# Loads of x with 128 rows per batch instead of 112, the last 16 rows zero

## The chip, the cores and the metric

The kernel runs on one core of a Trainium2 chip. The metric is the device time of one execution in microseconds (us); less is better. Between the two kernels, the median of three runs each is compared.

## What is computed

x has 8 batches of 112 rows of 256 float32 values (896 rows in all). A gated attention over a context and a gated mixture of experts are added to it one after the other. Cut to what matters:

```python
def _layernorm(x): m, v = mean(x), var(x); return (x - m) / sqrt(v + 1e-5)

def xattn(x, ctx):                       # x (8, 112, 256), ctx (8, 375, 256)
    h = einsum('eth,efh->etf', x, ctx)
    return einsum('etf,efh->eth', gelu(h), ctx)

def ffn(x, gate_w, gate_b, w1, b1, w2, b2):
    xf = x.reshape(-1, 256)
    top1 = argmax(xf @ gate_w.T + gate_b, axis=-1)      # one of 8 experts
    for e in range(8):
        y = relu(xf @ w1[e].T + b1[e]) @ w2[e].T + b2[e]
        out = out + where(top1 == e, y, 0)
    return out

x = x + tanh(g_xattn) * xattn(_layernorm(x), ctx_1024)
x = x + tanh(g_ffn)   * ffn(_layernorm(x), ...)
```

## The kernel before, in words

The program has two stages. The first one goes over the 8 batches b; each batch is one tile of 112 rows, a row to a partition. The tile of x lives in `x2[0:112, b, X0:RAW]`; `x2` is 128 partitions by 8 batches by 268 floats (4 floats ahead for mean, variance, 1/std and variance plus eps, 256 of x, 8 for the logits of the gate).

For a batch the work is, in this order: VectorE takes the statistics of x (`stats_x`, L564 and L566); GpSimd makes the inverse deviation (L285, L288); VectorE normalises (`norm_x`, L570); TensorE turns the tile (`turn_xn`, L900) and ScalarE copies it out of PSUM (L449); TensorE makes the scores against the turned context (`scores`, L910, 6 matmuls) and the gate's share from x (`x_logits`, L919, 2 matmuls); ScalarE takes the gelu (L457) and copies shares of the gate (`x_share`, L469; `gate_share`, L463); TensorE multiplies with the context's rows (`attend`, L928, 3 matmuls); VectorE adds the result to x (`add_attention`, L582) and takes the second statistics; GpSimd makes the second inverse deviation; ScalarE's queue stores the 112 rows with their statistics into a table in DRAM (`store_x2`, L474).

TensorE's order is written out by hand (L1005 to L1022): scores(0), turn(1), x_logits(0), and then for each b: scores(b+1), x_logits(b+1), turn(b+2), attend(b). x_logits(b) waits, from b = 2 on, until `add_attention` of batch b-2 is done, since it writes the same PSUM bank (L917). VectorE's order is also by hand (L671 to L711): statistics and normalisation of batches 0 to 2, statistics of batches 3 and 4, normalisation of batch 3, and only then `add_attention(0)`. GpSimd makes 1/std of batches 0 and 1, then a row of constants (L324 to L352), then 1/std of batch 2 and on.

The second stage gathers the rows of each expert from the table by indirect DMA (L381), runs nine blocks of 128 rows through the two matrices of their expert (`up`, L978; `down`, L987), and scatters the result (L386).

All big loads are issued by the SP queue, in the order in which they stand in the code (L243 to L258): x of batch 0, turned context of batch 0 (`load_context_T`, L231), x of 1, turned context of 1, x of 2, context rows of 0 (`load_context_rows`, L234), then **the rest of x, batches 3 to 7, in one load (L249)**, turned context of 2, context rows of 1 and of 2, whole contexts of 3 to 7 (`load_context`, L228), experts 0 and 1. SP issues experts 2 to 7 only after the first gathers have landed (L260 to L267). Each of the loads of x has a semaphore of its own; batches 3 to 7 share `x_in[3]`.

The loads of x move 112 rows: 3 loads of 112 rows of 1,024 bytes, and one load of 112 rows of 5 x 268 x 4 = 5,360 bytes (batches 3 to 7 laid out as `x2` has them, with the pads). All other loads of SP have 128 rows: 3,000 bytes a row for a turned context, 3,168 for context rows, 6,168 for a whole context, 8,192 for an expert's matrix.

Of the kernel before, what the change touches and what calls it, by code (L numbers as in the profile page):

```python
# [19 lines left out]
P = 128  # L20
# [10 lines left out]
B, S, D = 8, 112, 256  # L31
CTX = 375
E, H = 8, 1024
# [6 lines left out]
MEAN, VAR, RSTD, VEPS, X0 = 0, 1, 2, 3, 4  # L40
RAW = X0 + D
# [5 lines left out]
HEAD = 3  # L47
# [9 lines left out]
def gated_cross_attention_moe(nc, x, x_rest, ctx, small, w1t, w2t, b2, out):  # L57
    x2_dram = nc.dram_tensor("x2_rows", (TOKENS, ROW), F32, kind="Internal").ap()
    with ExitStack() as stack:
        def sb(name, shape, dt=F32):  # L60
            return stack.enter_context(nc.sbuf_tensor(name, shape, dt))
# [4 lines left out]
        def sem(name):  # L66
            return stack.enter_context(nc.semaphore(name))
# [27 lines left out]
        x2 = sb("x2", [P, B, ROW + E])  # L95
# [81 lines left out]
        x_in = [sem("x_in0"), sem("x_in1"), sem("x_in2"), sem("x_in3")]  # L177
# [47 lines left out]
        @block.sync  # L225
        def _(sp):
            def load_context(b):
                sp.dma_start(cxs[:, b, :], ctx[b]).then_inc(cx_in[b], 16)  # L228

            def load_context_T(b):  # L230
                sp.dma_start(cxT[:, b, :], ctx[b, :, 0:KD * CTX]).then_inc(cxT_in[b], 16)  # L231

            def load_context_rows(b):
                sp.dma_start(cx[:, b, :], ctx[b, :, KD * CTX:CW]).then_inc(cx_in[b], 16)  # L234

            def load_expert(e):
                sp.dma_start(w1[:, e, :], w1t[e]).then_inc(w1_in[e], 16)
                sp.dma_start(w2[:, e, :], w2t[e]).then_inc(w2_in[e], 16)

            def load_x(b):  # L240
                return sp.dma_start(x2[0:S, b, X0:RAW], x[b * S:(b + 1) * S])  # L241

            load_x(0).then_inc(x_in[0], 16)  # L243
            load_context_T(0)
            load_x(1).then_inc(x_in[1], 16)
            load_context_T(1)
            load_x(2).then_inc(x_in[2], 16)
            load_context_rows(0)
            sp.dma_start(x2[0:S, HEAD:B, :], x_rest).then_inc(x_in[3], 16)  # L249
            load_context_T(2)  # L250
            load_context_rows(1)
            load_context_rows(2)
            for b in range(3, B):
                load_context(b)

            load_expert(0)
            sp.dma_start(b2b[:, 0:D], b2[0:D].partition_broadcast(P)).then_inc(b2_in[0], 16)
            load_expert(1)  # L258

            sp.wait_ge(xnT_done, B)  # L260
            sp.wait_ge(xgT_done, 1)
            sp.wait_ge(first_in[1], 16)
            sp.wait_ge(xg_in[0], 16)
            load_expert(2)
            sp.dma_start(b2b[:, D:E * D], b2[D:E * D].partition_broadcast(P)).then_inc(b2_in[1], 16)
            for e in range(3, E):
                load_expert(e)  # L267
# [905 lines left out]
```

## Time and profile before

| what | us |
|---|---|
| median of 3 runs (lowest to highest) | 112.1 (110.88 to 112.54) |
| the profiled execution's own time | 111.79 |
| its span in the trace | 110.0 |
| outside the span | 1.79 |
| TensorE matmul busy | 100.7 (92% of the span) |
| VectorE busy | 53.5 (49%) |
| GpSimd busy | 39.9 (36%) |
| ScalarE busy | 28.6 (26%) |

The span is the stretch from the first to the last recorded instruction; all times in rows count from its start. "PE" is TensorE's matmul side, "PEld" its weight load, DVE is VectorE, ACT ScalarE, POOL GpSimd, SP the sync engine that issues the big loads; a q behind a name is the queue of that engine. L910 is line 910 of the kernel. The names in the rows are those of memory tensors: `x` is the tile `x2`, `region` the tile that holds the contexts, `w` the experts' matrices (in whose last parts the normalised x and the gelu lie for a time), `bank` is PSUM.

### The profile page before, as it was taken

The page shows a single profiled execution, that of the slowest core. Times are in us where ns is not written, and L with a number is a line of the kernel's source. Part 1 is how long each engine was busy: PE and PEld are TensorE (multiplying, and loading weights), DVE is VectorE, ACT ScalarE, POOL GpSimd, SP SyncE. Part 2 cuts the span into 40 slices and gives each one's busy share as a digit, 9 for nine tenths or more (in the row PEclk, how much of TensorE's full clock was granted, in tenths as well). Part 3 has the DMA queues.
Part 4 walks back from the last instruction along what each step waited for, and adds up shares of the span by engine and source line. Part 5 has one row for each costly group of instructions (what it writes and reads, how often), then busy time and mean ns, then how long its engine had stood idle before and what let it go on. Part 6 is the DMA issues. An engine that isn't in the chain of part 4 may idle for free.

```text
span 110.0 us, 2150 instructions
## 1 busy us (share of the span) xinstructions
PE 100.7 (92%) x704; PEld 92.7 (84%) x705; DVE 53.5 (49%) x204; ACT 28.6 (26%) x91; POOL 39.9 (36%) x97
## 2 busy tenths in 40 slices
PE   5999899999999997799999999999999999999900
PEld 5998669999988895799989999899999998998600
DVE  0461578669689884796555332344133241333010
ACT  5616143212351440152302303223032140220000
POOL 3276386353664937700330557030030030300330
PEclk9999999999999999999999999999999999999996
DMA  3999999999995202599999999999992010010101
GB/s 80 316 331 246 404 419 422 404 427 426 413 414 202 86 0 65 128 352 359 368 416 402 419 420 365 415 426 426 432 419 114 7 44 0 0 40 6 46 19 35
DMA packets 6734, 28.36 MB, mean 258 GB/s; under 512 B 1149, under 2 KB 2511, under 8 KB 4672
## 3 DMA queue, kind: packets, MB, share of 16 engines
q1 hardware_dynamic: 4688, 25.09, 58.2%
q0 software_dynamic: 864, 2.12, 6.3%
q10 hardware_dynamic: 1168, 0.98, 2.8%
q8 instruction: 7, 0.11, 0.4%
q14 instruction: 7, 0.06, 0.1%
HBM read 26.33 MB, written 2.11 MB: 259 GB/s over the span
## 4 chain that ended last, share of the span: by engine, by line
PE 71%; DMA 11%; DVE 6%; issue 3%; POOL 2%; SPq 2%; ACTq 0%; ACT 0%; POOLq 0%; DVEq 0%
PE bank L978 29%; PE bank L987 26%; DMA x<-in_x_rest 8%; PE bank L928 6%; PE bank L910 5%; DMA region<-x_rows,from_row 3%; PE bank L960 2%; PE bank L919 2%; DVE x L582 1%; SPq L241 1%; PE bank L900 1%; POOL out_rows L386 1%; DVE stats L589 1%; SPq L231 1%; DVE region L791 1%
## 5 line engine op out<-in xcount | busy, mean ns | idle before, releaser
L978 PE MATMUL bank<-region,w 128*128 128x128 f32 x288 | 34.7, 277 | 0.3 <-ACT region L485 0.3
L978 PEld LDWEIGHTS bank<-region,w 128*128 128x128 f32 x288 | 33.8, 192 | 0.8 <-ACT region L485 0.4
L987 PE MATMUL bank<-w,region 128*128 128x256 f32 x144 | 32.6, 379 | 0.0
L987 PEld LDWEIGHTS bank<-w,region 128*128 128x128 f32 x144 | 26.7, 190 | 3.2
L520 ACT ACTIVATE region<-bank,smalls 128x128 f32<-128x128 f32 x40 | 12.5, 363 | 39.9 <-PE bank L978 38.5
L386 POOL DMA_INDIRECT out_rows<-region,to_row x9 | 8.9, 989 | 33.9 <-DVE region L813 32.4
L797 DVE TENSOR_SCALAR region<-bank,smalls 128x128 f32<-128x128 f32 x32 | 9.7, 346 | 13.8 <-PE bank L978 13.4
L381 POOL DMA_INDIRECT region<-x_rows,from_row x9 | 9.3, 1032 | 15.7 <-DMA region<-x_rows,from_row 12.2
L813 DVE SCALAR_TENSOR_TENSOR region<-bank,tg,region 128x256 f32<-128x256 f32 (+1 forms) x9 | 4.4, 484 | 19.0 <-PE bank L987 19.0
L910 PEld LDWEIGHTS bank<-xnT,region 128*125 128x125 f32 x96 | 11.4, 188 | 2.2 <-issue 1.6
L910 PE MATMUL bank<-xnT,region 128*125 128x120 f32 x96 | 12.0, 275 | 0.8 <-issue 0.7
L928 PE MATMUL bank<-region,w 125*112 125x264 f32 x48 | 12.1, 388 | 0.0
L928 PEld LDWEIGHTS bank<-region,w 125*112 125x112 f32 x48 | 7.8, 177 | 1.5
L457 ACT ACTIVATE w<-bank 125x336 f32<-125x336 f32 x8 | 3.6, 450 | 12.0 <-PE bank L910 12.0
L994 PE MATMUL bank<-still 128*128 128x128 f32 x22 | 5.1, 419 | 1.1 <-DVE still L671 1.1
L582 DVE SCALAR_TENSOR_TENSOR x<-bank,tg,x 112x264 f32<-112x264 f32 x8 | 3.9, 488 | 3.5 <-PE bank L928 3.5
L791 DVE TENSOR_SCALAR region<-region 128x256 f32<-128x256 f32 (+1 forms) x8 | 3.6, 452 | 3.6 <-DMA region<-x_rows,from_row 3.6
L994 PEld LDWEIGHTS bank<-still 128*128 128x128 f32 x22 | 4.6, 318 | 0.8 <-DVE still L671 0.8
L564 DVE BATCH_NORM_STATS2 stats<-x 112x6 f32<-112x256 f32 x8 | 3.4, 422 | 3.7 <-DMA x<-in_x 2.1
L570 DVE TENSOR_SCALAR w<-x,mv 112x256 f32<-112x256 f32 x8 | 3.3, 418 | 3.7 <-POOL mv L288 3.7
L288 POOL TENSOR_TENSOR x<-x,power 112x1 f32<-112x1 f32 x8 | 4.5, 561 | 0.6
L288 POOL TENSOR_TENSOR mv<-mv,power 112x1 f32<-112x1 f32 x8 | 4.4, 553 | 0.6
(118 smaller groups left out, 85.7 us busy)
## 6 DMA issues: line engine op xcount, KB each, us to landing
w<-in_w1t SPq DMA_DIRECT2D x8, 1024.0 KB, 23.3
w<-in_w2t SPq DMA_DIRECT2D x8, 1024.0 KB, 26.5
region<-in_ctx SPq DMA_DIRECT2D x5, 771.0 KB, 13.2
region<-in_ctx SPq DMA_DIRECT2D x3, 396.0 KB, 9.1
region<-in_ctx SPq DMA_DIRECT2D x3, 375.0 KB, 4.2
x_rows<-x ACTq DMA_DIRECT2D x8, 113.8 KB, 6.4
b2b<-in_b SPq DMA_DIRECT2D x1, 896.0 KB
x<-in_x_rest SPq DMA_DIRECT2D x1, 586.2 KB, 8.3
```

The source lines that it names most:

```text
L288: return pool.tensor_tensor(v[:, 2:3], v[:, 3:4], power[0:S, :], ALU.pow)
L381: return pool.indirect_dma_start(out=to, out_offset=None, in_=x2_dram, in_offset=bass.IndirectOffsetOnAxis(ap=idx, axis=0), bounds_check=T ...
L386: return pool.indirect_dma_start(out=out, out_offset=bass.IndirectOffsetOnAxis(ap=idx, axis=0), in_=rows, in_offset=None, bounds_check=TOK ...
L520: act.activation(hidT[:, q, 2 * k + r, :], hT_ps[k][:, r * P:(r + 1) * P], ACT.Relu, bias=b1[:, bass.ds(e * KH + 2 * k + r, 1)]).then_inc( ...
L582: dve.scalar_tensor_tensor(out=x2[0:S, b, X0:ROW + E], in0=at_ps[b % 2][0:S, 0:DL], scalar=tg[0:S, 0:1], in1=x2[0:S, b, X0:ROW + E], op0=A ...
L791: dve.tensor_scalar(xgn[:, q, :], rows[:, X0:ROW], rows[:, MEAN:MEAN + 1], rows[:, RSTD:RSTD + 1], ALU.subtract, ALU.mult).then_inc(xgn_ok, 1)
L797: dve.tensor_scalar(hidT[:, q, 2 * k + r, :], hT_ps[k][:, r * P:(r + 1) * P], b1[:, bass.ds(e * KH + 2 * k + r, 1)], 0.0, ALU.add, ALU.max ...
L910: mm = pe.matmul(sc_ps[b % 2][0:CR, c * SL:(c + 1) * SL], cxT[:, b, k * CTX + c * CR:k * CTX + (c + 1) * CR], xnT[:, b % 2, k * SL:(k + 1) ...
L928: mm = pe.matmul(at_ps[b % 2][0:S, 0:DL], gel[0:CR, b % 2, c * S:(c + 1) * S], cx[0:CR, b, c * DL:(c + 1) * DL], start=(c == 0), stop=(c = ...
L978: mm = pe.matmul(hT_ps[k][:, part % 2 * P:(part % 2 + 1) * P], w1[:, e, n * H + part * P:n * H + (part + 1) * P], xgT[:, j % 2, n * P:(n + ...
L987: mm = pe.matmul(y[:, 0:D], hidT[:, q, part, :], w2[:, e, part * D:(part + 1) * D], start=(part == 0), stop=(part == KH - 1))
L994: pe.matmul(sc_ps[1][:, 0:P], still[:], still[:], start=True, stop=True)
```

## The change

The host pads each batch of x from 112 to 128 rows with zeros, and all four loads of x write 128 partitions instead of 112. So 3 loads have 128 rows of 1,024 bytes and one has 128 rows of 5,360 bytes. Nothing that computes is touched: every instruction still works on `x2[0:S]`, 112 rows.

```diff
             def load_x(b):
-                return sp.dma_start(x2[0:S, b, X0:RAW], x[b * S:(b + 1) * S])
+                return sp.dma_start(x2[:, b, X0:RAW], x[b])
...
-            sp.dma_start(x2[0:S, HEAD:B, :], x_rest).then_inc(x_in[3], 16)
+            sp.dma_start(x2[:, HEAD:B, :], x_rest).then_inc(x_in[3], 16)
...
     arrays = {
-        "x": np.ascontiguousarray(np.asarray(x)[0:HEAD]).reshape(HEAD * S, D),
+        "x": np.ascontiguousarray(np.pad(np.asarray(x)[0:HEAD], ((0, 0), (0, P - S), (0, 0)))),
         "x_rest": np.ascontiguousarray(np.pad(np.asarray(x)[HEAD:B].transpose(1, 0, 2),
-                                                 ((0, 0), (0, 0), (X0, E)))),
+                                                 ((0, P - S), (0, 0), (X0, E)))),
```

## Rows read from the trace of the kernel before

**Rows 1.** The page's busy time by engine, and the span in 40 slices of 2.75 us
```profile
PE 100.7 (92%) x704; PEld 92.7 (84%) x705; DVE 53.5 (49%) x204; ACT 28.6 (26%) x91; POOL 39.9 (36%) x97
...
DMA  3999999999995202599999999999992010010101
GB/s 80 316 331 246 404 419 422 404 427 426 413 414 202 86 0 65 128 352 359 368 416 402 419 420 365 415 426 426 432 419 114 7 44 0 0 40 6 46 19 35
```

**Rows 2.** The chain that ended last: start us, us, what
```profile
3.58 8.30 DMA x<-in_x_rest
...
11.91 0.44 DVE stats L564
...
13.81 0.50 DVE x L582
...
14.36 0.56 PE bank L919 x4
14.91 0.24 PE bank L900 x2
15.16 1.34 PE bank L928 x6
16.50 0.10 issue
16.60 1.54 PE bank L910 x12
18.14 0.30 PE bank L919 x4
...
40.48 3.37 DMA region<-x_rows,from_row
```

**Rows 3.** Timeline: start us, us, engine line op out<-in xcount [idle before <-releaser]
```profile
8.80 0.34 POOL L350 TENSOR_SCALAR_AFFINE_SELECT upto<-upto 128x81 f32<-128x81 f32 x1
...
9.41 0.55 POOL L288 TENSOR_TENSOR mv<-mv,power 112x1 f32<-112x1 f32 x1
...
10.00 0.41 DVE L570 TENSOR_SCALAR w<-x,mv 112x256 f32<-112x256 f32 x1 [2.01 <-POOL mv L288]
...
10.72 1.50 PE L928 MATMUL bank<-region,w 125*112 125x264 f32 x6
...
11.91 0.43 DVE L564 BATCH_NORM_STATS2 stats<-x 112x6 f32<-112x256 f32 x1 [1.49 <-DMA x<-in_x_rest]
...
12.70 1.54 PE L910 MATMUL bank<-xnT,region 128*125 128x120 f32 x12 [0.48 <-issue]
...
13.65 0.19 ACT L463 ACTIVATE region<-bank 125x24 f32<-125x24 f32 x1 [2.37 <-DMA region<-in_ctx]
```

**Rows 4.** SP's loads by line, us from issue to landing: L249, L231, L234, L228
```profile
L249 SPq DMA_DIRECT2D x<-in_x_rest x1: 429/429/429, 3.6 to 3.6; - x1
DMA to landing us min/median/max: 8.3/8.3/8.3
L231 SPq DMA_DIRECT2D region<-in_ctx x3: 418/429/429, 1.2 to 4.1; - x3
DMA to landing us min/median/max: 3.7/4.2/8.6
L234 SPq DMA_DIRECT2D region<-in_ctx x3: 429/491/858, 3.1 to 5.1; - x3
DMA to landing us min/median/max: 6.7/9.1/9.6
L228 SPq DMA_DIRECT2D region<-in_ctx x5: 434/447/651, 6.0 to 8.1; - x5
DMA to landing us min/median/max: 10.5/13.2/16.9
```

**Rows 5.** Stretches: last three columns are TensorE's granted clock, DMA share, GB/s
```profile
2.00:6.50 4.50, 4.47 (x25) 4.30 (x24) 1.86 (x7) 2.79 (x6) 1.24 (x4) 1.00 0.96 308
8.00:10.50 2.50, 2.31 (x23) 2.21 (x21) 0.41 (x1) 1.29 (x5) 2.02 (x14) 1.00 0.99 240
6.50:11.50 5.00, 4.81 (x40) 4.57 (x41) 1.56 (x5) 2.01 (x7) 3.45 (x22) 1.00 1.03 287
12.50:18.00 5.50, 5.08 (x37) 4.34 (x38) 4.29 (x15) 1.32 (x5) 3.74 (x12) 1.00 1.03 423
```

**Rows 6.** The DMA queue of SP: packets, MB, share of 16 engines
```profile
q1 hardware_dynamic: 4688, 25.09, 58.2%
```

## The prediction

> **What bounds the kernel now.** I read the page first. Matmul is busy for 92% of the span, and the 40 slices show the DMA engines full in slices 1 to 11, at some 400 to 430 GB/s from slice 4 on, but at only 316, 331 and 246 GB/s in slices 1 to 3 [rows 1]. The chain of waits says what the first 16 us hang on: SP issues the load of the rest of x at 3.58 us, it lands 8.30 us later, VectorE starts the statistics of batch 3 at 11.91, reaches `add_attention(0)` at 13.81, and this releases TensorE's x_logits(2) at 14.36 [rows 2]. From 16.60 on each batch is TensorE on TensorE (scores, x_logits, turn, attend) until the last batches; the rest of the chain (routing, the gather at 40.48, the nine blocks) hangs on the end of that run [rows 2]. So what the change gains or loses by 16.60 arrives at the end nearly whole; batches 4 to 7 of x, which come with the same load, are wanted long after it has landed.
>
> Three things reach TensorE late before 16.60. (a) scores(2) starts at 12.70, though attend(0) was through at 10.72 + 1.50 = 12.22 [rows 3]: the turned context of batch 2, issued at 4.06 (the last of the three at L231) with the longest landing, 8.6 us, lands at 12.66 [rows 4]. (b) x_logits(2) waits for `add_attention(0)` until 14.31; its four pieces take 0.56 us where batch 3's take 0.30 [rows 2]. (c) 0.10 us of "issue" at 16.50, ahead of scores(3) [rows 2]: the first whole context, issued at 5.96, lands 10.5 us later, at 16.46 [rows 4]. Context rows of batch 1 land shortly before 13.65, where ScalarE takes them [rows 3]. All of these loads stand behind the rest of x in SP's queue.
>
> **What the DMA stretches say.** In the stretch from 8.0 to 10.5 the engines are busy for 0.99 of the time but move 240 GB/s; from 12.5 to 18.0 they are as busy (1.03) and move 423 [rows 5]. That is 15.0 against 26.4 GB/s per engine. The slow stretch is where the rows of L249 are under way: issued at 3.58, landed at 11.88. Rows of contexts of 3,168 and 6,168 bytes go at 423, so a row of 5,360 bytes isn't slow by its length. What sets this load apart is that it has 112 rows where the fast ones have 128. I take the row count, that is, how the rows fall on engines and partitions, as the cause.
>
> **The change part by part.** (1) *More bytes.* 16 rows more in each load: 3 x 16 x 1,024 + 16 x 5,360 = 134,912 bytes. At 423 GB/s that is 0.32 us of the queue, at the 308 GB/s of the early stretch 0.44 [rows 5]. Only 16 x 1,024 bytes, 0.04 to 0.05 us, stand ahead of batch 0's statistics; I put +0.05 on the front of the chain. (2) *Issue.* The same four instructions on SP; 0.43 us for the 112-row L249 and 0.42 to 0.43 for the 128-row L231 [rows 4], so nothing. (3) *No compute* is added or taken away, no wait, no instruction on ACT or POOL; their instructions stay at 112 rows. (4) *Rate of the loads.* From 6.5 to 11.5 the queue moved 287 x 5.0 = 1.435 MB [rows 5]; at 423 that takes 3.39 us, so 1.61 us are lost there. If all of it belongs to the 112-row shape, what stands behind the rest of x lands 1.61 - 0.32 = 1.29 us earlier. If only half does, 0.80 - 0.32 = 0.48 us earlier. If none does, 0.32 to 0.44 later. I take the upper end, or close to it.
>
> **What that is worth to TensorE.** attend(0) doesn't move forward: it stands behind turn(2), which needs norm_x(2) at 10.00, which waits for GpSimd's L288 at 9.41, and that stands behind GpSimd's constants, the last big one at 8.80 [rows 3]. So attend(0) still ends at 12.22, and with (1) at 12.27. From there, with the full gain:
> - The turned context of batch 2 is there at 12.66 - 1.29 = 11.4, so scores(2) starts at about 12.3 instead of 12.70 and ends, after 1.54 us, at 13.85.
> - The rest of x is there at 10.6. From that landing to `add_attention(0)` it is now 13.81 - 11.88 = 1.93 us, so it starts at about 12.5 and is through at 13.0, before 13.85. x_logits(2) then runs in 0.30 us, not 0.56, and turn(3) takes 0.24: attend(1) starts at about 14.4 instead of 15.16. It also needs the context rows of batch 1: 13.65 less 1.3, in time.
> - attend(1) ends at 14.4 + 1.34 = 15.75, the whole context of batch 3 is there at 16.46 - 1.29 = 15.2, so scores(3) starts at about 15.75 to 15.8 instead of 16.60: 0.80 to 0.85 us earlier.
>
> With half the gain the landings are 12.2 for the turned context, 11.4 for the rest of x and 16.0 for context 3; TensorE follows the same path until it waits for that context, scores(3) starts at 16.05, 0.55 us earlier. So the gain saturates: between 0.55 and 0.85 us over a wide span of causes; I take 0.75. Contexts 4 to 7 are no closer bound: one takes 789,504 bytes / 423 GB/s = 1.87 us of the queue, while TensorE spends over 3 us on a batch (1.54 + 0.30 + 0.24 + 1.34) [rows 2]. In the second stage SP's loads start behind the gathers, so they shift with the chain, and the slices show them done (slice 30, some 83 us) well ahead of the end [rows 1].
>
> **The sum.** Against the profiled execution: 111.79 - 0.75 = 111.0. That execution lies 0.3 us under the median of the runs shown (112.1; less 0.75 it is 111.35). I forecast 111.2 for the median after, between the two. That is a change of 0.7%; a measurement of this kernel can tell about 2% from no change, so the forecast is "within 2%".
>
> **Rivals.** *A, slower: only bytes.* The slow stretch has another cause (the place in DRAM, the queue beside it), the shape changes nothing, and the 16 added rows are just more to move. SP's queue has 4,688 packets [rows 6]. Its loads have 4,160 rows in all (448 of x, 768 of single context parts, 640 of whole contexts, 2,048 of experts, 256 of the biases), and 33 loads with one small packet from each of 16 engines are 528 more: 4,688 exactly. So the 112-row loads are on 16 engines already, and no idle engine is waiting to be used; that speaks for A. By the skill's rule on the engine count (same page and section as above) this trace agrees, and 128 rows give each engine 8 rows for 7. Price: the turned context lands at 13.0 to 13.1, and each later landing slips by 0.32 to 0.44, up to context 3 at 16.8 to 16.9, so scores(3) starts 0.3 to 0.4 later. Time: 112.1 to 112.2 against the profiled 111.79, 112.5 against the median. It decides if a row of the rest of x keeps its cost: then 8 rows take 8/7 of what 7 took. Against it: 240 GB/s at full share in just that stretch.
>
> *B, hidden.* The load of x gets fast, but the turned context of batch 2 and what follows keep their own slowness, their landings staying near 12.66 and 16.46. Then `add_attention(0)` comes in time, attend(1) ends 0.3 us earlier, and TensorE stands still until 16.46 for context 3: 0.1 us gained, 111.7. Against it: they share the queue with it, and only the stretch as a whole is slow.
>
> *C, more.* The early stretch, 308 GB/s from 2.0 to 6.5 [rows 5], has three 112-row loads in it and speeds up too; batch 0 and 1 of x land up to 0.2 us earlier, which moves GpSimd's constants and attend(0) by as much. 0.95 to 1.05 us gained, 110.8. Against it: rows of 1,024 bytes may be slow simply by being short, and the first landing is mostly latency.
>
> **How the numbers follow.** Forecast (0.55 to 0.85 us gained) 0.50, C 0.12, B 0.15, A 0.20, and 0.03 for what I don't see. The runs of before spread from 0.4 above to 1.2 below their median, more than all the cases lie apart, so the range is set by both: 110.8 less 0.5 is 110.3 at the low end, and A's 112.5 at the high end. None of the mechanisms comes near 2.2 us (2%), so over 2% faster is 0.03 and over 2% slower 0.02.
>
> **What would show it.** Right: the DMA stretch from 8.0 to 10.5 above 350 GB/s, L249's landing at 10.8 us or before (7.2 us or less from issue, now 8.3), no idle time before the statistics of batch 3 beyond some 0.3 us, scores(2) at about 12.3 and scores(3) at about 15.8. The chain then no longer passes through the load of the rest of x but through GpSimd's constants and TensorE. SP's queue must count 4,688 + 64 = 4,752 packets. Wrong: the stretch stays at 240 GB/s and L249 lands later than 11.9 (A), or it lands early and scores(3) still starts at 16.5 (B), or a wait that is new takes TensorE's time between 16.6 and 29.

## The result, and the profile after

The changed kernel takes 110.41 us (median of 20 runs, 110.03 to 110.73) against 111.22 us (20 runs, 110.49 to 112.54): ratio 0.9924, 95% interval 0.990 to 0.9948. It is faster by 0.8 us. That is within 2%, and clear of noise with this many runs. A ratio here and below is formed from the fast executions of both kernels alone (those within 1.5% of the fastest one of their kernel), so it need not equal the quotient of the medians. The forecast was 111.2 us, 0.7% faster. The profiled execution took 110.65 us with a span of 108.8, 1.14 us less than the profiled one of before; that one lies 0.6 us above its own median, so the medians lie closer together.

The page after, in the lines that answer to [rows 1] and [rows 6]:

```profile
PE 100.2 (92%) x704; PEld 93.2 (86%) x705; DVE 53.4 (49%) x204; ACT 28.4 (26%) x91; POOL 39.9 (37%) x97
...
DMA  3999999999995103599999999999992010010100
GB/s 74 288 376 404 423 422 412 411 426 419 381 416 187 49 0 98 148 392 355 382 408 428 416 404 391 409 421 431 431 397 79 0 44 0 0 40 6 48 26 28
...
q1 hardware_dynamic: 4752, 25.22, 58.0%
```

Slice 3, 246 GB/s before, is at 404. SP's queue has 4,752 packets, the 64 added rows and nothing else. The stretches after, with the columns of [rows 5]:

```profile
2.00:6.50 4.50, 4.50 (x23) 4.50 (x23) 1.77 (x7) 2.76 (x6) 0.95 (x3) 1.00 0.97 292
...
8.00:10.50 2.50, 2.31 (x24) 2.25 (x22) 0.45 (x3) 0.94 (x4) 2.29 (x17) 1.00 1.01 405
6.50:11.50 5.00, 4.81 (x41) 4.60 (x41) 2.31 (x9) 1.86 (x8) 3.90 (x23) 1.00 1.02 404
```

From 8.0 to 10.5 the engines are as busy as before and move 405 GB/s instead of 240; the early stretch is no faster than it was (292 against 308). The trace's record of single packets says the same of the rows themselves: a row of 5,360 bytes of the big load takes 318 ns on average before and 213 ns after. What that does to the landings, as [rows 4] has them:

```profile
L249 SPq DMA_DIRECT2D x<-in_x_rest x1: 432/432/432, 3.6 to 3.6; - x1
DMA to landing us min/median/max: 6.0/6.0/6.0
L231 SPq DMA_DIRECT2D region<-in_ctx x3: 426/432/583, 1.2 to 4.1; - x3
DMA to landing us min/median/max: 3.9/4.4/6.5
L228 SPq DMA_DIRECT2D region<-in_ctx x5: 438/452/620, 6.0 to 8.2; - x5
DMA to landing us min/median/max: 8.5/11.2/15.8
```

The rest of x lands 6.0 us after its issue (8.3 before), the turned context of batch 2 6.5 (8.6), the whole context of batch 3 8.5 (10.5): each about 2 us earlier in this pair of profiles. (How much of that is this pair and how much the change comes below.) The chain after goes through none of them. Its pieces around the place where it used to hang, and the first one behind the last attend (columns as in [rows 2]):

```profile
11.17 1.34 PE bank L928 x6
12.51 1.31 PE bank L910 x12
13.82 0.30 PE bank L919 x4
14.12 0.25 PE bank L900 x2
14.37 1.34 PE bank L928 x6
15.71 1.30 PE bank L910 x12
...
28.62 0.50 DVE x L582
...
39.35 3.34 DMA region<-x_rows,from_row
```

TensorE runs without a gap from attend(0) on; scores(3) comes in the chain at 15.71 where it came at 16.60. The same step of VectorE behind attend(6) starts at 28.62; in the chain of before it is this row:

```profile
29.75 0.50 DVE x L582
```

So 0.89 us are won at scores(3) and 1.13 at the end of the stage; the other 0.24 is that scores(3) takes 1.30 us of the chain in a row of matmuls that doesn't stop, and 1.54 behind a gap [rows 2]. In the timeline most of this is overlap: there scores(3) starts at 15.54, 0.16 us before attend(1) is through, and takes 1.47 us, against 1.54 before. From there the distance is kept: the gather of the second stage starts at 39.35 for 40.48.

The spread of the runs shrank too, from 2.05 us to 0.70.

### The profile page after: what moved, and what is told of

It is laid out like the page before. It is cut to its first block, busy times and chain, and to the rows that moved or that the text cites. A ratio compares the mean times of both kernels' runs of the same rounds, so it can differ in the third digit from the quotient of the medians.

```text
span 108.8 us, 2150 instructions
## 1 busy us (share of the span) xinstructions
PE 100.2 (92%) x704; PEld 93.2 (86%) x705; DVE 53.4 (49%) x204; ACT 28.4 (26%) x91; POOL 39.9 (37%) x97
## 3 DMA queue, kind: packets, MB, share of 16 engines
q1 hardware_dynamic: 4752, 25.22, 58.0%
## 4 chain that ended last, share of the span: by engine, by line
PE 83%; DVE 5%; DMA 3%; issue 3%; POOL 2%; ACTq 0%; ACT 0%; POOLq 0%; DVEq 0%
PE bank L978 29%; PE bank L987 26%; PE bank L910 9%; PE bank L928 7%; PE bank L994 5%; DMA region<-x_rows,from_row 3%; PE bank L900 2%; PE bank L919 2%; PE bank L960 2%; DVE x L582 1%; POOL out_rows L386 1%; DVE stats L589 1%; DVE region L791 1%; DVE cand L620 1%; POOL x L288 1%
## 5 line engine op out<-in xcount | busy, mean ns | idle before, releaser
L491 ACT ACTIVATE region<-bank 128x256 f32<-128x256 f32 x8 | 3.1, 384 | 5.9 <-PE bank L960 5.9
```

## The experiments

Ratios are to the kernel before, timed beside the others of that series; brackets hold the 95% interval. Each kernel has one profile, of one execution.

**1. Which load is it?** Two kernels make one half of the change each. Only the big load:

```diff
-            sp.dma_start(x2[0:S, HEAD:B, :], x_rest).then_inc(x_in[3], 16)
+            sp.dma_start(x2[:, HEAD:B, :], x_rest).then_inc(x_in[3], 16)
```

> Only the load of batches 3 to 7 (L249) gets 128 rows; batches 0 to 2 keep 112. Theory S (the 112-row shape of the big load is what is slow): L249 lands about 6.0 us after its issue as in the changed kernel (8.3 before), DMA stretch 8.0 to 10.5 above 390 GB/s, ratio to the kernel before 0.990 to 0.994, like the whole change or up to 0.2 us better, since batches 0 and 1 keep their fewer bytes. Rival E (each of the four loads gives its share): only part of the gain, ratio 0.995 to 0.998.

Only the three small ones:

```diff
-                return sp.dma_start(x2[0:S, b, X0:RAW], x[b * S:(b + 1) * S])
+                return sp.dma_start(x2[:, b, X0:RAW], x[b])
```

> Only the loads of batches 0, 1 and 2 get 128 rows; L249 keeps 112. Theory S: L249 still lands 8.2 to 8.5 us after issue, DMA stretch 8.0 to 10.5 at 230 to 260 GB/s, ratio 0.999 to 1.003 (49 KB more to move and nothing won). Rival E: L249's landing falls to about 7.5 us and the ratio is 0.995 to 0.998.

And the changed kernel beside them:

> The changed kernel as it is, for comparison on the same chip. Both theories: ratio 0.990 to 0.995; if TensorE's slow matmuls between 5.5 and 6.7 us (L1002 took 0.55 us on the weight side against 0.30 before) belong to the change, they are there again; if they are chance, scores(0) starts at about 6.45 here.

Measured: big load alone 110.17 us, 0.9956 [0.9924, 0.9989]; small loads alone 111.27 us, 1.0049 [1.0022, 1.0077]; whole change 110.34 us, 0.9976 [0.9950, 1.0001]. The kernel before had a good series there (median 110.89, and one execution at 175.32 us that is left out of the ratios), which lifts all the ratios: those of the big load and of the whole change were expected at 0.990 to 0.994 and 0.990 to 0.995, that of the small loads at 0.999 to 1.003, and all three lie above. By the ratio alone the big load would have fallen into Rival E's range (0.995 to 0.998), and the interval of the whole change touches 1. What decides is the kernels of this series side by side: with 128 rows in the big load 110.17 and 110.34 us, with 112 rows 110.89, 111.27 and 111.33 (experiment 2). The stretches from 8.0 to 10.5 of the big load alone (first row) and of the small loads alone (second row):

```profile
8.00:10.50 2.50, 2.31 (x22) 2.25 (x21) 0.46 (x3) 1.21 (x5) 2.29 (x18) 1.00 0.99 357
```

```profile
8.00:10.50 2.50, 2.31 (x24) 2.25 (x22) 0.48 (x2) 0.94 (x4) 2.20 (x16) 1.00 0.98 244
```

The slow stretch follows the big load. Two expectations of the profiles were missed in part. In the profile of the big load alone L249 landed 7.5 us after issue, not 6.0, and its stretch was at 357, not above 390; that profile is of an execution of 111.30 us, 1.1 us above the median of its kernel, in which context 3 landed at 16.0 and held scores(3) until 16.07. So the wait can come back with 128 rows. In that of the small loads alone it landed after 7.3 us, which was Rival E's number, though the rate of its stretch stayed where theory S had it, at 244. So one landing is a poor witness: it tells only when the last row was done. With 112 rows it came 8.3, 7.8 and 7.3 us after issue in three profiles with the load in its place, with 128 rows 6.0, 6.1, 6.6, 6.9 and 7.5. The rate of the stretch separates the two without an overlap in the same eight profiles: 236 to 244 against 357 to 405. So does the time of single packets. A 5,360-byte row of the big load takes 317 to 337 ns on average with 112 rows and 213 to 224 with 128. And a row of the turned context of batch 2, which stands behind it in the queue and has 128 rows in every kernel, takes 184 to 189 ns behind the 112-row load and 119 to 137 behind the 128-row one: the loads behind are slowed as well.

**2. Is it the place in DRAM?** The arrays padded as in the change, the loads cut back to 112 rows:

```diff
-                return sp.dma_start(x2[:, b, X0:RAW], x[b])
+                return sp.dma_start(x2[0:S, b, X0:RAW], x[b, 0:S])
...
-            sp.dma_start(x2[:, HEAD:B, :], x_rest).then_inc(x_in[3], 16)
+            sp.dma_start(x2[0:S, HEAD:B, :], x_rest[0:S]).then_inc(x_in[3], 16)
```

> The arrays on the host are padded to 128 rows as in the changed kernel, but all four loads move 112 rows. Theory S: as before the change, L249 lands 8.2 to 8.5 us after issue, ratio 0.998 to 1.002. Rival P (the place of the rows in DRAM, moved by the padding, made the load fast): L249 lands in about 6 us and the ratio is that of the change, 0.990 to 0.994.

```profile
8.00:10.50 2.50, 2.31 (x24) 2.25 (x23) 0.41 (x1) 1.15 (x5) 1.84 (x13) 1.00 1.01 236
```

111.33 us, 1.0043 [1.0004, 1.0083], and 236 GB/s in the stretch: the padding on the host doesn't bring the gain. Two expectations were missed, neither towards Rival P: L249 landed 7.8 us after issue (8.2 to 8.5), and the ratio is above 0.998 to 1.002. The loads move the same rows as in the kernel before, so 0.4% is how far a like kernel can come out in this series; the small loads' 0.5% above is no more than that. What counts is how many rows the load has.

**3. The load by itself.** The last term of the argument, the cost of a 112-row load, was measured alone. Behind the last expert, the changed kernel issues twelve more loads, each waiting for the one before it. It was executed once:

```diff
+            sp.wait_ge(w2_in[E - 1], 16)
+            sp.dma_start(x2[0:128, HEAD:B, :], x_rest[0:128]).then_inc(probe, 16)
+            sp.wait_ge(probe, 16)
+            sp.dma_start(x2[0:112, HEAD:B, :], x_rest[0:112]).then_inc(probe, 16)
+            sp.wait_ge(probe, 32)
...
```

> The changed kernel with twelve more loads of SP at the end, after the last expert has landed, each alone on the queue (a wait for the landing between them): 5,360-byte rows in this order of row counts: 128, 112, 128, 112, 96 (rows 0 to 95), 64, 112 (rows 16 to 127), 120, 16, 127, then 1,024-byte rows: 128 and 112. Theory S in its strong form (a 112-row load meets itself at the ports): the 112-row load alone takes as long as the 128-row one or longer, by up to 0.7 us. Rival N (it is slow only where loads with another split of rows run beside it): the 112-row load alone takes 0.2 us less than the 128-row one, in proportion to its rows (7 rows of 0.206 us per engine against 8). Both: 120 rows on 15 engines as long as 128, 127 rows far longer, if the engine count follows the row count.

SP's instructions in the timeline (start us, us); each one starts when the load before it has landed:

```profile
84.07 0.33 SPq L271 DMA_DIRECT2D x<-in_x_rest  x1
87.55 0.34 SPq L273 DMA_DIRECT2D x<-in_x_rest  x1
91.95 0.34 SPq L275 DMA_DIRECT2D x<-in_x_rest  x1
95.46 0.33 SPq L277 DMA_DIRECT2D x<-in_x_rest  x1
99.95 0.33 SPq L279 DMA_DIRECT2D x<-in_x_rest  x1
103.92 0.52 SPq L281 DMA_DIRECT2D x<-in_x_rest  x1
107.92 0.32 SPq L283 DMA_DIRECT2D x<-in_x_rest  x1
112.26 0.38 SPq L285 DMA_DIRECT2D x<-in_x_rest  x1
117.30 0.32 SPq L287 DMA_DIRECT2D x<-in_x_rest  x1
119.51 0.23 SPq L289 DMA_DIRECT2D x<-in_x_rest  x1
147.53 0.35 SPq L291 DMA_DIRECT2D x<-in_x  x1
149.62 0.31 SPq L293 DMA_DIRECT2D x<-in_x  x1
```

The differences of the starts are the times:

| rows of 5,360 bytes | us from start to next start | per-engine share if even |
|---|---|---|
| 128 | 3.48 and 3.51 | 8 rows |
| 112 (0 to 111) | 4.40 and 4.49 | 7 rows |
| 112 (16 to 127) | 4.34 | 7 rows |
| 96 | 3.97 | 6 rows |
| 64 | 4.00 | 4 rows |
| 120 | 5.04 | 8 rows on 15 engines |
| 16 | 2.21 | 1 row |
| 127 | 28.02 | 127 rows on one engine |

Theory S holds in its strong form, and Rival N falls: alone on SP's queue, 112 rows take 0.8 to 1.0 us longer than 128, though they are an eighth fewer; up to 0.7 was expected. Alone on the queue isn't alone on the engines: the second stage still scatters its results, and 45 to 51 packets of that (some 0.1 MB) fall beside the loads of rows 0 to 111, 96 and 64, against 0 and 3 beside the two 128-row loads. The clean witness is the load of rows 16 to 127: no packet of another queue beside it, and 4.34 us. Even 64 rows, with the scatter beside them, take 0.5 us more than 128. The expectation that 120 rows on 15 engines take as long as 128 was missed by 1.5 us, and nothing ran beside those. With about 2.0 us that don't depend on size (an estimate from 16 rows: 2.21, of which one row is 0.2), 128 rows move in 1.5 us and 112 in 2.4. The packet record has the same in the time of a single row, on average: 238 and 241 ns in the 128-row loads, 275 to 295 in the three of 112, 306 in that of 96, 350 in that of 64, 336 in that of 120, and 207 in that of 127. So for the load itself the change is worth 0.8 to 1.0 us net, as the 86 KB more are already paid in it. The 1,024-byte rows show nothing: the wait behind the 128-row load was 1.7 us (2.09 from start to start), and that behind the 112-row one 1.7 as well.

The Trainium skill's page DMA: Bandwidth & Descriptors ("Why a DMA increments its semaphore by 16 and not by 1") says that the number of engines is the largest divisor of the row count up to 16, with 127 rows on one engine. The 28.02 us agree: 127 rows x 0.203 us (5,360 bytes at the 26.4 GB/s per engine of [rows 5]) are 25.8 us, and the fixed 2.0 make it 27.8. But for 112, 96 and 64 rows the same rule gives 16 engines and would predict less time than for 128; these rows deny that the count of engines is the whole story. SBUF — State Buffer ("Door 1: The DMA port swizzle") has 64 partitions reach only half of 16 ports. By this 64 rows put 8 rows on each of 8 ports, as 128 rows do on 16, and should take as long, about 3.5 us (an estimate from the 128-row loads); the measured 4.00, with the scatter beside it, agrees that half the rows bring no time and leaves 0.5 us over. That two engines met at one port was not observed, as no view shows ports.

**4. A split without padding.**

```diff
-            sp.dma_start(x2[0:S, HEAD:B, :], x_rest).then_inc(x_in[3], 16)
+            sp.dma_start(x2[0:96, HEAD:B, :], x_rest[0:96]).then_inc(x_in[3], 16)
+            sp.dma_start(x2[96:S, HEAD:B, :], x_rest[96:S]).then_inc(x_in[3], 16)
...
-                dve.wait_ge(x_in[min(b, HEAD)], 16)
+                dve.wait_ge(x_in[min(b, HEAD)], 32 if b >= HEAD else 16)
```

> From the kernel before: the load of batches 3 to 7 cut into two, rows 0 to 95 and rows 96 to 111, no row added. Theory S with the split by blocks of rows: 96 rows are 6 to an engine, which straddle groups of partitions too, so the stretch stays slow, L249's landing stays above 7.5 us from the first issue, ratio 0.998 to 1.003. Rival M (what counts is that the row count is a multiple of 32): both pieces run at full speed, the second lands at about 6.2 us from the first issue, ratio 0.990 to 0.995, with 86 KB less to move than in the change.

```profile
8.00:10.50 2.50, 2.04 (x19) 1.89 (x18) 0.46 (x2) 1.52 (x6) 2.08 (x15) 1.00 1.00 219
```

111.40 us, 1.0023 [0.9977, 1.0070]; the stretch moves 219 GB/s, the slowest of all. A row of these two loads takes 349 ns on average. A multiple of 32 rows isn't enough, as 96 rows alone show. (The first piece landed 6.9 us from its issue, under the 7.5 expected; the second, which ends the load, 7.7 us from its own, 8.2 from the first.)

**5. What is the delay of the queue worth?** The changed kernel with the same load issued once more behind the first, into a free place:

```diff
             sp.dma_start(x2[:, HEAD:B, :], x_rest).then_inc(x_in[3], 16)
+            sp.dma_start(b2b[0:128, D:D + 1340], x_rest[0:128].rearrange("p b n -> p (b n)")).then_inc(extra, 16)
...
+            sp.wait_ge(extra, 16)
             sp.dma_start(b2b[:, D:E * D], b2[D:E * D].partition_broadcast(P)).then_inc(b2_in[1], 16)
```

> The changed kernel with one load more behind the rest of x: the same 128 rows of 5,360 bytes once more, into a part of b2b that is free until much later. It delays the turned context of batch 2 and all that follows by 686 KB / 423 GB/s = 1.6 us, while the rest of x itself still comes early. Theory Q (the whole queue behind the load counts): context 3 is back at about 16.3 to 16.9 us, scores(3) starts at 16.4 to 16.9, the gain is gone, ratio to the kernel before 0.998 to 1.004. Rival B (only the landing of the rest of x counts): ratio stays at 0.991 to 0.996.

The same with `0:112` in place of `0:128`:

> As the kernel with the extra 128-row load, but the extra load has 112 rows, 86 KB less. By its bytes it would cost 0.2 us less than the 128-row one. Theory S (shape): it costs 0.7 to 1.2 us more of the queue (alone a 112-row load took 4.4 us from issue to the next instruction, a 128-row one 3.5), so context 3 lands at 17.2 us or later and the kernel is 0.5 to 1.0 us slower than the one with the extra 128-row load: ratio 1.004 to 1.012.

With 128 rows: 111.58 us, 1.0035 [1.0004, 1.0067]. With 112 rows, 86 KB less: 112.29 us, 1.0118 [1.0072, 1.0165]. TensorE at scores(2) and scores(3) with 128 rows, then with 112 (both views end before scores(3) does):

```profile
13.09 1.47 PE L913 MATMUL bank<-xnT,region 128*125 128x120 f32 x12
...
16.84 1.32 PE L913 MATMUL bank<-xnT,region 128*125 128x120 f32 x10 [0.40 <-issue]
```

```profile
13.37 1.54 PE L913 MATMUL bank<-xnT,region 128*125 128x120 f32 x12 [1.26 <-issue]
...
17.27 0.99 PE L913 MATMUL bank<-xnT,region 128*125 128x120 f32 x7 [0.47 <-issue]
```

Both landed in their expected ranges. The first undoes the gain with bytes alone although x itself comes early (6.6 us from issue): context 3 lands at 16.8 and sets the start of scores(3) again. So it isn't the landing of x alone that counts (this experiment's Rival B). Behind the extra 112-row load context 3 lands at 17.2. The second is the price of the shape in its cleanest form: fewer bytes, and 0.71 us slower.

**6. Does the rest of x still set the pace?** In the changed kernel, its load moved behind the turned context of batch 2:

```diff
-            sp.dma_start(x2[:, HEAD:B, :], x_rest).then_inc(x_in[3], 16)
             load_context_T(2)
+            sp.dma_start(x2[:, HEAD:B, :], x_rest).then_inc(x_in[3], 16)
```

> The changed kernel with the load of batches 3 to 7 moved behind the turned context of batch 2, so that it comes 0.9 us later (384 KB / 423 GB/s) and that context 1.6 us earlier. Theory (the rest of x has slack now: add_attention(0) is through about 0.5 us before x_logits(2) wants it, and TensorE runs without a gap): within 0.002 of the changed kernel, ratio to the kernel before 0.990 to 0.998, x_logits(2) at most 0.4 us later. Rival (the landing of the rest of x still sets the pace): 0.5 us or more slower than the changed kernel, ratio 0.998 or above.

```profile
11.11 0.43 DVE L564 BATCH_NORM_STATS2 stats<-x 112x6 f32<-112x256 f32 x1 [0.68 <-DMA x<-in_x_rest]
...
13.01 0.49 DVE L582 SCALAR_TENSOR_TENSOR x<-bank,tg,x 112x264 f32<-112x264 f32 x1
...
13.55 0.47 PEld L919 LDWEIGHTS bank<-xnT 128*112 128x112 f32 x4 [0.18 <-DVE x L582]
```

110.39 us, 0.9933 [0.9909, 0.9957]. The changed kernel wasn't timed beside it; in its own series it had 110.34 to 110.41. VectorE waits for the rest of x again, `add_attention(0)` is at 13.01 for 12.62, and the weight load of x_logits(2) waits 0.18 us for it. Scores(3) still starts at 15.53 (15.54 in the changed kernel): there is slack, and this order uses it up.

**7. The best version, and what the small loads cost.** The kernel with only the big load at 128 rows, again, and the changed one in the same series:

> Only the load of batches 3 to 7 gets 128 rows, once more, now beside the changed kernel in the same call. If the 48 KB more of batches 0 to 2 cost something (theory F, 0.1 to 0.3 us at the front of the chain), this one is 0.001 to 0.003 faster than the changed kernel; if their better shape is worth something (rival G), it is 0.001 to 0.004 slower.

> The changed kernel once more, for comparison in the same call: ratio to the kernel before 0.990 to 0.998.

110.06 us, 0.9908 [0.9877, 0.9940], against 110.41 us, 0.9954 [0.9922, 0.9986]. It was the faster one in the first series too (110.17 against 110.34). The start of the statistics of batch 0 shows a possible reason: 2.96 to 3.07 us in the five profiles with 112 rows in the small loads, 3.10 to 3.50 in the eight with 128. The rows of the kernel with the big load alone, and of the changed kernel:

```profile
3.07 0.43 DVE L564 BATCH_NORM_STATS2 stats<-x 112x6 f32<-112x256 f32 x1 [2.00 <-DMA x<-in_x]
```

```profile
3.10 0.43 DVE L564 BATCH_NORM_STATS2 stats<-x 112x6 f32<-112x256 f32 x1 [2.04 <-DMA x<-in_x]
```

This speaks for theory F, with 0.17 and 0.35 us between the medians; the intervals overlap in both series, so its size isn't settled, and that the 0.1 us at batch 0 reaches TensorE isn't shown. What attend(0) follows is batch 1: it starts 5.5 us behind the start of that batch's statistics in ten of the thirteen profiles, and that lies between 5.03 and 5.66 with 112 rows in the small loads and between 5.12 and 6.25 with 128. Nothing speaks for padding the small loads, so they are the part of the change to leave out.

## Why the prediction was right

*Where the gain is.* The chain was read as hanging on the queue up to 16.60 and then passing the shift on. Both held: 0.89 us at scores(3), 1.13 at the gather, 1.2 at the end of the span. The chain after doesn't name GpSimd's constants, as the forecast had it; it is TensorE on TensorE, though narrowly: norm_x(2), which stands behind the constants, is done 0.06 us before turn(2) starts.

*The term for the queue.* 1.61 us lost, 1.29 net, was the upper end and was taken nearly whole. In the profiled pair the landings came forward by 2.3, 2.1 and 2.0 us, but landings scatter by over a microsecond between executions with the same loads, so a single pair isn't a size. Over all profiles that have these loads in their places (three with 112 rows; six with 128, that of experiment 3 among them, whose extra loads come far behind) the rest of x lands 7.3 to 8.3 us after issue against 6.0 to 7.5, the turned context of batch 2 7.7 to 8.6 against 6.5 to 8.0, and context 3 at 15.7 to 16.5 against 14.5 to 16.0: between the means 1.0 to 1.2 us, close to the forecast's 1.29. Part of it is the load itself (0.8 to 1.0 us alone), part the slower rows behind it (184 to 189 ns for 119 to 137).

*Saturation.* The gain was put at 0.55 to 0.85 us, whatever the queue gave beyond half: 2 us at the landings of the profiled pair became 0.89 at scores(3), since TensorE had nothing left to wait for. Step by step: attend(0) through at 12.51 (forecast 12.27), scores(2) at 12.51 (12.3), attend(1) at 14.37 (14.4), scores(3) at 15.71 (15.75 to 15.8).

*The front, and luck in it.* +0.05 us for the added row bytes ahead of batch 0 was too little, and the wrong load: attend(0) is later by 0.29, and that comes from batch 1. Its statistics wait for x and start 0.28 us later, and GpSimd's constants and norm_x(2) with them. The two rows of after and of before:

```profile
5.50 0.43 DVE L564 BATCH_NORM_STATS2 stats<-x 112x6 f32<-112x256 f32 x1 [0.31 <-DMA x<-in_x]
```

```profile
5.22 0.43 DVE L564 BATCH_NORM_STATS2 stats<-x 112x6 f32<-112x256 f32 x1 [0.16 <-DMA x<-in_x]
```

In the second profile of the changed kernel they start at 5.19, and attend(0) is only 0.10 us later than before, so this is mostly the scatter of one landing. Two errors then cancelled: this one, and the 0.24 us of the chain that a score group without a gap ahead of it is shorter, which the forecast left out for scores(2). It left it out for scores(3) too, and nothing cancelled that: the profiled pair gains 1.13 us, more than the 0.85 at the upper end.

*Rivals.* A, only bytes, fell with the first profile after: the stretch is at 405, and experiment 2 rules out the place in DRAM. Its observation (16 engines were in use already) was right and decided nothing, for engines in use aren't engines at full rate. B, that the loads behind keep their own slowness, fell with the same profile: the turned context of batch 2 lands at 10.6 for 12.66, context 3 at 14.5 for 16.46. C, that the early stretch gains too, isn't borne out: 291 to 322 GB/s in the eight profiles with 128-row small loads, 296 to 308 in the five with 112, and batch 1's statistics start no earlier.

*The number.* 110.41 lies in the range 110.3 to 112.5, 0.1 us above its low end, and 0.8 under the forecast of 111.2. The reason is the level, not the difference: the three runs of before had a median of 112.1, and twenty have 111.22; less 0.75 that is 110.5. That it stayed in the range is luck in part, since the range was that wide for the scatter of before; by itself 110.41 would lie nearest to C's 110.8. What bears the forecast out is the difference of the medians: 0.81 us here, and 0.55 and 0.70 where the changed kernel was timed again, at ratios of 0.9924, 0.9976 and 0.9954.

*The spread.* With the 112-row load the runs spread over 2.05 us, without it over 0.70 (20 runs each); in the two later series with both it was 2.1 (without the one execution at 175.32) and 2.0 against 1.0 and 1.4. The fastest run of before, 110.05 to 110.49 in every series, is about as fast as the median of the changed kernel. This fits landings that vary (7.3 to 8.3 us for the 112-row load) and cost only when they are late enough to stop TensorE: in the profile with the landing at 7.3, scores(3) started at 15.80. It was not followed run by run.

## What to carry to other kernels

When the DMA engines are fully busy but move half of what they move elsewhere, look at the row count of the load in that stretch: here a large load of 112, 96 or 64 rows took longer than one of 128, and padding it on the host brought 0.7 and 1.0 us (medians of two series) for 86 KB. Pad the large loads that others queue behind; leave small ones that stand at the head of the chain as short as they are. Don't size a transfer by one landing: it scattered here by more than the change moved it, while the rate of the stretch and the time of a row separated the kernels in every profile. And size a gain by where the next limit stands: 2 us at the landings of one pair of profiles were worth 0.9 at scores(3).

## What the runs showed that was not expected

- A load of 64 rows takes 4.00 us and one of 128 rows of the same length 3.5; 120 rows take 5.04. Why is open.
- One 112-row load slows the 128-row load queued behind it: 184 to 189 ns for a 3,000-byte row instead of 119 to 137.
- TensorE's first microseconds differ between executions of like kernels. The weight load of the warm-up tile took 333 ns in the profile after still at 6.2 to 6.4 us and 192 ns in the profile before at 5.9 to 6.0, after the same twenty warm-up matmuls. The view of stretches gives a granted clock of 1.00 in both, so only the durations tell. It reaches scores(0) (6.79 for 6.45) and not attend(0), which hangs on the landing of batch 1. These are the rows from 5.5 us on, of after and of before:

```profile
L994 PEld LDWEIGHTS bank<-still x2: 333/333/333, 6.2 to 6.4; 128*128 128x128 f32 x2
```

```profile
L994 PEld LDWEIGHTS bank<-still x2: 192/192/192, 5.9 to 6.0; 128*128 128x128 f32 x2
```

It was slow at that point in five of the eight profiles with 128-row small loads and in none of the five with 112; the second profile of the changed kernel has it again. Whether the loads have a part in it stays open.
